# One-hots of the high digit built on partitions from digit rows that DMA spreads, then turned for the histogram

## The chip, the cores and the metric

The kernel runs on one core of a Trainium2 chip. The metric is the device time of one launch in microseconds (us). The engines are named as in the profile: PE is TensorE, DVE is VectorE, ACT is ScalarE, POOL is GpSimd, SP is SyncE. SP computes nothing; it issues DMAs, one after the other, in the order of its program.

## The reference, cut to what matters

2048 users have 200 history entries each, and an entry has three ids (0 to 999), each a row of one of three tables.

```python
ub = jnp.concatenate([table_i1[rec_his[:, :, 0]], table_i2[rec_his[:, :, 1]], table_i3[rec_his[:, :, 2]]], axis=2)
mask = rec_his[:, :, 0] == 0
att_in = jnp.concatenate([q, ub, q - ub, q * ub], axis=-1)
score = ((att_in @ w_att1.T + b_att1) @ w_att2.T + b_att2)[..., 0]
score = jnp.where(mask, 0.0, score)
browse = jnp.einsum('bl,ble->be', score, ub)
```

The score is linear in the history row, so it is a sum of three looked-up numbers per entry, and the weighted sum of rows is a histogram of scores over ids, multiplied by the tables. Behind it come two dense layers with batch statistics and a sigmoid.

## The kernel before, in words

**Lookup by digits.** An id is 25 times a high digit (40 values) plus a low digit (25 values). For 100 entries of one user (half a history) a one-hot of the high digit for three features, 120 wide, with 8 more rows in front, makes 128 (`HJ`). With the table's scores laid out as 128 rows (high digit) by 75 columns (low digit of three features) one matmul group looks all scores of the high digit up into `sel`. The 8 front rows hold the low digit and its square, and `far` rows in `scoretab` turn them into a huge negative number wherever the column is not the entry's low digit, so a maximum over the 25 columns picks the score.

**The histogram** (`add_scores`) is a matmul of the same one-hot, now with the 100 entries on partitions, by the low one-hot times the score in three bf16 parts (`scaled_lo`).

**Two layouts.** The lookup needs the high one-hot with 128 rows on partitions (`hiT`), the histogram with 100 entries on partitions (`onehot_hi`). DVE builds `onehot_hi` with one comparison (`onehot_high`), ACT adds the low-digit columns (`lo_rows`), and SP issues one DMA transpose per step that writes `hiT` (`turn_hi`). The digits themselves reach the 100 partitions by PE transposes of `digits_b` (tasks `digit`, kind 1 the high one, kind 0 the low one).

**Tiles, steps, slots.** A tile is 128 users (16 tiles), a step is 8 users or 16 half histories (16 steps a tile, 256 in all), and a slot is half a step. In a step DVE does `pick` (maximum over `sel`), `onehot_high` for the step two ahead (`AHEAD = 2`), `onehot_low`, the second `pick`, and `scale` for the step before. POOL turns the picked scores into three bf16 parts between `pick` and `scale`. PE does in each slot 24 matmuls of `read_scores`, some task, and 24 matmuls of `add_scores` for the slot `LAG = 5` back. In the last two and the first two steps of a tile SP also moves the next tile's score table (`place_scores`, five chunks of three DMAs each); twice a tile it loads ids (`load_rows`), once it keeps `x1`. All of these stand in SP's one queue with the transposes, and each waits there for its semaphores before the next is looked at.

Of the kernel before, what the change touches and what calls it, by code (L numbers as in the profile page):

```python
# [16 lines left out]
def build(nc, r_user, r_item, r_his, table_user, table_i1, table_i2, table_i3, w_att1, b_att1,  # L17
# [12 lines left out]
    POSP = 112  # L30
# [11 lines left out]
    RING = 6  # L42
# [5 lines left out]
    with ExitStack() as ctx:  # L48
# [16 lines left out]
        onehot_hi = sb("onehot_hi", [POSP, RING, PER, HJ], BF16)  # L65
        onehot_lo = sb("onehot_lo", [POS, 2, PER, NF, LP], BF16)
        scaled_lo = sb("scaled_lo", [POS, 2, PER, 3, U], BF16)
        hiT = sb("hiT", [128, 4, PER * POSP + 128 - POSP], BF16)
# [5 lines left out]
        digits = sb("digits", [POS, 2, 2, 2 * HALF, NF, 2], BF16)  # L74
        far_rows = sb("far_rows", [1, 3, LO], BF16)
# [4 lines left out]
        centre = sb("centre", [POS, 1])  # L80
# [3 lines left out]
        iota_i = sb("iota_i", [POS, HI], I32)  # L84
        iota_hi = sb("iota_hi", [POS, HI], BF16)
# [37 lines left out]
        x1_rows = nc.dram_tensor("x1_rows", [MH, 2, B], F32).ap()  # L123
        stats = raw_f[:, 0:72].rearrange("p (m q s) -> p m q s", m=3, q=4)
# [38 lines left out]
        hi_ready = sem("hi_ready")  # L163
        lo_ready = sem("lo_ready")
        hiT_in = [sem(f"hiT_in{i}") for i in range(4)]
        rim_zero = sem("rim_zero")
# [3 lines left out]
        lo_rows_ready = sem("lo_rows_ready")  # L170
# [33 lines left out]
        def ring_slot(n):  # L204

            return n % 5 if n < STEPS - 1 else RING - 1

        def sums_before(k, n):

            return 2 * k - (8 if 5 <= n < STEPS - 1 else 10 if n < 5 else 2 * STEPS - 2)  # L210

        def ring_used(k, n):

            return not isinstance(k, int) or sums_before(k, n) > 0

        prologue = (["attw"] + [("tableT", i) for i in range(7)] + [("digit", 1, 0), ("digit", 0, 0), "item", "query",
                                                                    "w1T", "w1uT", "w2T"])
        DIGITS0 = prologue.index(("digit", 0, 0)) + 1  # L220
# [8 lines left out]
        def split_bank(first, r):  # L229
# [8 lines left out]
        EVERY = {0: "item", 1: "query", 2: ("digit", 1, 1), 3: ("digit", 0, 1), FIN_SLOT + PARTS - 1: "finish",  # L238
                 FIN_SLOT + PARTS: "layer1", 19: "userT", 20: ("digit", 1, 0), 21: ("digit", 0, 0)}
        IN_FIRST = {s: w for s, w in EVERY.items() if w not in FIN}  # L240
        IN_LAST = {s: w for s, w in EVERY.items() if w not in ("item", "query", ("digit", 1, 0), ("digit", 0, 0))}
# [38 lines left out]
        def _(sp):  # L280
# [25 lines left out]
            sp.wait_ge(far_made, 3)  # L306
            for j in range(NF):
                sp.dma_start(far[0:1, j, :], far_rows[:, 0, :]).then_inc(far_in, 16)
                sp.dma_start(far[1 + 2 * j:2 + 2 * j, j, :], far_rows[:, 1, :]).then_inc(far_in, 16)
                sp.dma_start(far[2 + 2 * j:3 + 2 * j, j, :], far_rows[:, 2, :]).then_inc(far_in, 16)  # L310
# [5 lines left out]

            def turn_hi(t, n):
# [31 lines left out]
            def tile(t, last=False):  # L349
                for n in range(STEPS):  # L350
                    if n == 14 and not last:
                        place_scores(t + 1, 0)
                    if n + AHEAD < STEPS:
                        turn_hi(t, n + AHEAD)
                    elif not last:
                        turn_hi(t + 1, n + AHEAD - STEPS)
                    if n < 2:
                        place_scores(t, 3 + n)
                    if n in (2, 9) and not last:
                        load_rows(2 * t + 2 + n // 9)  # L360
# [8 lines left out]

            load_rows(1)  # L370
            for n in range(AHEAD):
                turn_hi(0, n)
# [12 lines left out]
        def _(pool):  # L385
# [61 lines left out]
            def step(t, n, last=False):  # L447
# [8 lines left out]
                if n == 3:  # L456

                    if not (isinstance(t, int) and t == 0):
                        await_ge(task_full, tasks_start(t) - 2)
                    gather_users(t, 2 * t + (3 if last else 4))  # L460
# [6 lines left out]
            chain(pool.iota(iota_i[:, :], pattern=[[1, HI]], base=1, channel_multiplier=0))  # L467
            chain(pool.tensor_copy(iota_hi[:, :], iota_i[:, :]))
# [7 lines left out]
            pool.tensor_scalar(far_rows[:, 1, :], column, 2.0 * FAR, None, ALU.mult).then_inc(far_made, 1)  # L476
            chain(pool.memset(ids_u[:, TILES:TILES + 1, :].bitcast(F32), 0.0))
# [28 lines left out]
        def _(pe):  # L506
# [6 lines left out]
            def hi_columns(s4, g):  # L513

                return onehot_hi[0:POS, s4, g, :]

            def read_scores(t, s):

                k = t * SLOTS + s
                if s % 2 == 0:  # L520
                    pe.wait_ge(hiT_in[s // 2 % 4], 16 * (t * (STEPS // 4) + s // 8 + 1))
# [6 lines left out]
                for c in range(8):  # L528
# [5 lines left out]
                    rows = hiT[0:HJ, s // 2 % 4, g * POSP:g * POSP + 128]  # L534
# [5 lines left out]
            def add_scores(t, s):  # L540

                k = t * SLOTS + s
                n = s // 2
                pe.wait_ge(scaled_ready, t * STEPS + n + 1)
                if not (isinstance(k, int) and k < 2):
                    pe.wait_ge(wsum_copied, k - 1)
                for i in range(6):
                    for b in range(4):
                        g = (s % 2) * 8 + 2 * b + i // 3
                        mm = pe.matmul(wsum_ps[:, s % 2, b * W:(b + 1) * W].rearrange("p (j v) -> p j v", j=NF),  # L550
                                       hi_columns(ring_slot(n), g),
# [22 lines left out]
            def task(what, seq, t, part=0, parts_n=1):  # L574
# [42 lines left out]
                elif name == "digit":  # L617

                    hb, kind = what[2], what[1]
                    await_ge(digits_b_ready, (t * 2 + hb) * 2 + 2 - kind)  # L620
                    src = digits_b[:, kind, :].rearrange("p (l f) -> p f l", f=NF)
# [35 lines left out]
            def slot(t, s, last=False):  # L657
# [6 lines left out]
                elif s in here:  # L664
                    what = here[s]
                    of = t
                    if what in ("item", "query", ("digit", 1, 0), ("digit", 0, 0)):
# [57 lines left out]
        def _(act):  # L725
# [39 lines left out]
            def task(what, seq, t):  # L765
# [18 lines left out]
                elif name == "digit":  # L784
                    kind, hb = what[1], what[2]
                    if not (isinstance(t, int) and t == 0):

                        if kind == 1:
                            act.wait_ge(hi_ready, (t - 1) * STEPS + 8 * hb + 8)
                        else:  # L790
                            act.wait_ge(lo_ready, (t - 1) * STEPS + 8 * hb + 8)
                    src = misc_b[0:POS, 0:2 * NF * HALF]
                    ins = act.activation(digits[:, hb, kind, :, :, :].rearrange("p g j d -> p j g d"),
# [47 lines left out]
            def lo_rows(t, n):  # L841

                k = t * STEPS + n
                hb, g0 = n // 8, (n % 8) * PER
                if n in (0, 8):

                    if isinstance(t, int) and t == 0 and n == 0:
                        act.wait_ge(task_copied, DIGITS0)
                    elif n == 0:
                        act.wait_ge(task_copied, tasks_start(t))  # L850
                    else:
                        act.wait_ge(task_copied, task_before(t, 3) + 1)

                if ring_used(k, n):
                    act.wait_ge(wsum_full, sums_before(k, n))
                low = digits[:, hb, 0, g0:g0 + PER, :, 0]
                rows = onehot_hi[0:POS, ring_slot(n), :, 1:1 + 2 * NF].rearrange("p g (j i) -> p g j i", i=2)
# [334 lines left out]
```

## Time and profile before

| | |
|---|---|
| median of 3 runs | 1602.13 us (1595.31 to 1602.28) |
| the profiled execution, its own time | 1588.28 us |
| its span | 1586.5 us |
| busy: DVE, PE, POOL, ACT | 1438.8, 1330.5, 1132.5, 716.7 us |
| mean granted clock of PE | 0.921 of full speed |
| DMA | 194.21 MB in 510281 packets |

Busy time counts computing instructions. Instructions that issue DMAs are not in it, so SP has no row in that table, although it can be occupied all the time; its occupation is read from the durations of its DMA instructions (queue SPq). The share of a DMA queue is the time that its packets took, over 16 DMA engines and the stretch; packets that overlap count twice, so it can pass 100%.

### The profile page before, as it was taken

The page shows a single profiled execution, that of the slowest core. Times are in us where ns is not written, and L with a number is a line of the kernel's source. Part 1 is how long each engine was busy: PE and PEld are TensorE (multiplying, and loading weights), DVE is VectorE, ACT ScalarE, POOL GpSimd, SP SyncE. Part 2 cuts the span into 40 slices and gives each one's busy share as a digit, 9 for nine tenths or more (in the row PEclk, how much of TensorE's full clock was granted, in tenths as well). Part 3 has the DMA queues.
Part 4 walks back from the last instruction along what each step waited for, and adds up shares of the span by engine and source line. Part 5 has one row for each costly group of instructions (what it writes and reads, how often), then busy time and mean ns, then how long its engine had stood idle before and what let it go on. Part 6 is the DMA issues. An engine that isn't in the chain of part 4 may idle for free.

```text
span 1586.5 us, 67332 instructions
## 1 busy us (share of the span) xinstructions
PE 1330.5 (84%) x26911; PEld 1225.9 (77%) x26911; DVE 1438.8 (91%) x1453; ACT 716.7 (45%) x1633; POOL 1132.5 (71%) x1669
## 2 busy tenths in 40 slices
PE   5687988889797987979788897988879798997965
PEld 4577878879797877969788797888879787887861
DVE  7799898999999998999989999898999999998955
ACT  5353453535354353635445353443535344452217
POOL 3588586787877777687767878686786878777730
PEclk9799999999999998999899899999989999998966
DMA  2768676585757777585676858486676857678720
GB/s 30 146 109 156 96 145 123 121 158 111 156 108 145 121 129 140 109 158 109 135 116 120 158 111 157 98 139 125 121 157 102 157 106 138 128 124 147 118 68 0
DMA packets 510281, 194.21 MB, mean 122 GB/s; under 512 B 484005, under 2 KB 491797, under 8 KB 510045
## 3 DMA queue, kind: packets, MB, share of 16 engines
q1 hardware_dynamic: 492454, 162.61, 57.8%
q10 hardware_dynamic: 15448, 26.51, 6.5%
q8 instruction: 221, 3.62, 0.9%
q0 software_dynamic: 2144, 1.36, 0.7%
q14 instruction: 14, 0.11, 0.0%
HBM read 8.45 MB, written 1.44 MB: 6 GB/s over the span
## 4 chain that ended last, share of the span: by engine, by line
POOL 62%; issue 24%; PE 4%; DVE 4%; POOLq 2%; DMA 2%; SPq 1%; ACT 1%; ACTq 0%; DVEq 0%
POOL score L431 16%; POOL score L436 14%; POOL score_r L440 10%; POOL parts L441 7%; POOL parts L444 7%; POOL parts L437 4%; POOL item_rows L409 2%; POOL user_rows L417 2%; DMA hiT<-onehot_hi 2%; PE sel L536 1%; PE wsum_ps L550 1%; PE misc L638 1%; DVE score_j L1000 1%; DVE scoretab L1086 1%; PE sel L714 1%
## 5 line engine op out<-in xcount | busy, mean ns | idle before, releaser
L536 PE MATMUL sel<-scoretab,hiT 128*128 128x75 bf16 x12288 | 560.3, 206 | 146.8 <-DMA hiT<-onehot_hi 117.4
L536 PEld LDWEIGHTS sel<-scoretab,hiT 128*128 128x128 bf16 x12288 | 521.4, 103 | 208.6 <-issue 141.7
L550 PE MATMUL wsum_ps<-scaled_lo,onehot_hi 100*128 100x75 bf16 x12288 | 554.3, 204 | 69.6 <-DVE scaled_lo L1012 68.8
L550 PEld LDWEIGHTS wsum_ps<-scaled_lo,onehot_hi 100*128 100x128 bf16 x12288 | 509.1, 102 | 85.9 <-DVE scaled_lo L1012 78.9
L1012 DVE TENSOR_TENSOR scaled_lo<-onehot_lo,parts 100x3744 bf16<-100x3744 bf16 x256 | 539.5, 2107 | 22.0 <-POOL parts L444 19.0
L755 ACT ACTIVATE wsum_ring<-wsum_ps 128x300 f32<-128x300 f32 x512 | 215.0, 420 | 676.0 <-PE wsum_ps L550 666.0
L431 POOL TENSOR_TENSOR score<-score_j 100x16 f32<-100x16 f32 x256 | 306.9, 1199 | 293.6 <-DVE score_j L1000 292.8
L1000 DVE TENSOR_REDUCE score_j<-sel 100x24 f32<-100x600 f32 x512 | 395.8, 773 | 36.5 <-PE sel L536 34.2
L968 DVE TENSOR_TENSOR onehot_hi<-digits,iota_hi 100x1920 bf16<-100x1920 bf16 x256 | 297.8, 1164 | 47.6 <-PE wsum_ps L550 46.9
L762 ACT ACTIVATE scores_b<-acc 128x512 bf16<-128x512 f32 (+1 forms) x318 | 256.1, 805 | 43.8 <-PE acc L569 24.5
L436 POOL TENSOR_TENSOR score<-score,score_j 100x16 f32<-100x16 f32 x256 | 229.3, 896 | 22.0
L986 DVE TENSOR_TENSOR onehot_lo<-digits,iota_lo 100x1248 bf16<-100x1248 bf16 x256 | 211.8, 827 | 0.0
L440 POOL TENSOR_TENSOR score_r<-score,parts 100x16 f32<-100x16 f32 x256 | 168.8, 659 | 20.0
L444 POOL TENSOR_TENSOR parts<-score_r,parts 100x32 bf16<-100x32 f32 x256 | 123.2, 481 | 20.1
L441 POOL TENSOR_TENSOR parts<-score,parts 100x32 bf16<-100x32 f32 x256 | 128.2, 501 | 0.0
L638 PE MATMUL misc<-weightsum,table_blk 128*96 128x128 f32 x800 | 113.9, 286 | 4.6 <-DMA weightsum<-wsum_ring 4.6
L569 PE MATMUL acc<-queryT,tableT 97*128 97x128 f32 x758 | 111.1, 287 | 0.6 <-issue 0.6
L562 PE MATMUL acc<-scores_b,minus_identb 128*128 128x512 bf16 (+1 forms) x212 | 101.5, 479 | 0.1
L638 PEld LDWEIGHTS misc<-weightsum,table_blk 128*96 128x96 f32 x800 | 94.3, 169 | 4.8 <-issue 4.8
L409 POOL DMA_INDIRECT item_rows<-in_L_rec_table_i_dram,ids_now x51 | 81.9, 1605 | 20.5 <-POOL ids_now L403 12.5
L569 PEld LDWEIGHTS acc<-queryT,tableT 97*128 97x128 f32 x758 | 94.0, 193 | 0.7 <-issue 0.7
L858 ACT ACTIVATE onehot_hi<-digits,centre 100x48 bf16<-100x48 bf16 x256 | 91.6, 358 | 0.0
(155 smaller groups left out, 671.0 us busy)
## 6 DMA issues: line engine op xcount, KB each, us to landing
scoretab<-scores_b SPq DMA_DIRECT2D x144, 187.5 KB
weightsum<-wsum_ring ACTq DMA_DIRECT2D x128, 125.0 KB
weightsum<-wsum_ring ACTq DMA_DIRECT2D x64, 150.0 KB
scoretab<-scores_b SPq DMA_DIRECT2D x96, 93.8 KB
raw<-in_r_rec_his_dram SPq DMA_DIRECT2D x32, 150.0 KB
hiT<-onehot_hi SPq DMA_TRANSPOSE x256, 4.8
x_rows<-x_tile SPq DMA_DIRECT2D x14, 100.0 KB
scores_b<-x_rows SPq DMA_DIRECT2D x1, 1400.0 KB
```

The costliest lines, as they stand in the source:

```text
L431: pool.tensor_tensor(score_2[:, :], score_j[:, p2, :, 0], score_j[:, p2, :, 1], ALU.add).then_inc(parts_step, 1)
L436: pool.tensor_tensor(score[:, :], score_2[:, :], third, ALU.add)
L440: pool.tensor_tensor(score_r[:, :], score[:, :], parts[:, p2, :, 0, 0], ALU.subtract)
L441: pool.tensor_tensor(parts[:, p2, :, 1, :], twice(score[:, :]), parts[:, p2, :, 0, :], ALU.subtract).then_inc(parts_step, 1)
L444: pool.tensor_tensor(parts[:, p2, :, 2, :], twice(score_r[:, :]), parts[:, p2, :, 1, :], ALU.subtract).then_inc(parts_ready, 1)
L536: mm = pe.matmul(o, rows, scoretab[0:HJ, s // 16, :, b, i, :], start=(i == 0), stop=(i == 2))
L550: mm = pe.matmul(wsum_ps[:, s % 2, b * W:(b + 1) * W].rearrange("p (j v) -> p j v", j=NF), hi_columns(ring_slot(n), g), scaled_lo[:, n % 2 ...
L638: mm = pe.matmul(misc[0:E, 0:TILE].rearrange("p (w b) -> p w b", w=4), table_blk[:, lo, :, :].rearrange("p j e -> p (j e)"), weightsum[0:H ...
L762: act.activation(scores_b[:, :, stage, slice(*ROUNDS[r])], split_bank(first, r), ACT.Copy).then_inc(split_copied, 1)
L968: dve.tensor_tensor(onehot_hi[0:POS, ring_slot(n), :, HB:].rearrange("p g (j v d) -> p g j v d", j=NF, d=2), digits[:, hb, 1, g0:g0 + PER, ...
L1000: dve.tensor_reduce(score_j[:, n % 2, g0:g0 + 8, :].rearrange("p (q c) j -> p q (c j)", q=2), sel[0:POS, 2 * (s % 2):2 * (s % 2) + 2, 0:4 ...
L1012: ins = dve.tensor_tensor(scaled_lo[:, n % 2, :, :, :].rearrange("p q i (u d) -> p (q i) u d", d=2), onehot_lo[:, n % 2, :, :, :].rearrang ...
```

## The change

1. ACT copies both digits, and the low digit's centred square, from interleaved to feature by feature (`spread_digits`, `digits_f`), and SP stores them in DRAM (`store_digits`, `digit_store`): twice a tile.
2. In each step SP loads each feature's high digit, 1600 numbers, onto 40 partitions at once: three DMAs whose source repeats one row 40 times (`load_high`, `high_rows`).
3. DVE compares each partition with its own number (`high_of`) in one `tensor_scalar`, which gives `hiT` at once, with no transpose.
4. The 6 low-digit rows come by one more DMA from `digit_store` into `hiT` (`load_front`), behind the comparison.
5. The DMA transpose goes the other way, `hiT` to `onehot_hi`, 128 by 2048 instead of 112 by 2048, and is waited for by `add_scores` instead of `read_scores`.
6. `lo_rows` and the PE and ACT tasks for the high digit go away.

```diff
+            def store_digits(h):
+                await_ge(spread_ready, KINDS * (h + 1))
+                sp.dma_start(digit_store[bass.ds(h, 1), :, :, :].rearrange("o r p l -> p (o r) l"),
+                             digits_f[:, :, :, :].rearrange("p k f l -> p (k f) l")).then_inc(rows_out, 16)
+            def load_high(t, n):
+                if n % 8 == 0:
+                    await_ge(rows_out, 16 * (h + 1))
...
+                    await_ge(hi_made, k - 1)
+                users = slice((n % 8) * PER, (n % 8) * PER + PER)
+                for j in range(NF):
+                    sp.dma_start(high_rows[hi_first(j):hi_first(j) + HI, n % 2, :],
+                                 digit_store[bass.ds(h, 1), FEAT[j]:FEAT[j] + 1, users, :].rearrange("o r p l -> (o r) (p l)")
+                                 .to_broadcast([HI, PER * POS])).then_inc(high_in[n % 2], 16)
+            def load_front(t, n):
+                await_ge(hi_made, k + 1)
+                sp.dma_start(hiT[1:1 + 2 * NF, n % RING, :, 0:POS],
+                             digit_store[bass.ds(2 * t + n // 8, 1), NF:KINDS * NF, users, :]
+                             .rearrange("o r p l -> (o r) p l")).then_inc(front_in[n % RING], 16)
             def turn_hi(t, n):
-                await_ge(hi_ready, k + 1)
-                await_ge(lo_rows_ready, k + 1)
-                if not (isinstance(k, int) and k < 4):
-                    await_ge(sel_full, 2 * k - 6)
-                sp.dma_start(hiT[:, n % 4, 0:PER * POSP].rearrange("p (g l) -> p g l", g=PER),
-                             onehot_hi[:, ring_slot(n), :, :].rearrange("p g h -> p (g h)"), transpose=True
-                             ).then_inc(hiT_in[n % 4], 16)
+                await_ge(front_in[n % RING], 16 * (t * (STEPS // RING) + n // RING + 1))
+                if not (isinstance(k, int) and k < RING):
+                    await_ge(wsum_full, 2 * (k - RING) + 2)
+                sp.dma_start(onehot_hi[:, n % RING, :, :], hiT[:, n % RING, :, :].rearrange("p g l -> p (g l)"),
+                             transpose=True).then_inc(hi_in[n % RING], 16)
             def tile(t, last=False):
                 for n in range(STEPS):
+                    for ahead, load in ((AHEAD, load_front), (2 + AHEAD, load_high), (1, turn_hi)):
+                        if n + ahead < STEPS:
+                            load(t, n + ahead)
...
             def onehot_high(t, n):
-                dve.tensor_tensor(onehot_hi[0:POS, ring_slot(n), :, HB:].rearrange("p g (j v d) -> p g j v d", j=NF, d=2),
-                                  digits[:, hb, 1, g0:g0 + PER, :, :].unsqueeze(3)
-                                  .to_broadcast([POS, PER, NF, HI // 2, 2]),
...
+                dve.wait_ge(high_in[n % 2], NF * 16 * (t * (STEPS // 2) + n // 2 + 1))
...
+                dve.tensor_scalar(hiT[:, n % RING, :, 0:POS], high_rows[:, n % 2, :].rearrange("p (g l) -> p g l", g=PER),
+                                  high_of[:, 0:1], None, ALU.is_equal).then_inc(hi_made, 1)
```

On SP, a step in the middle of a tile's loop body was this before (ISA and REGISTER_ALU rows are waits and the arithmetic for them and for addresses):

```order
L284 REGISTER_ALU
L284 ISA [waits hi_ready,lo_rows_ready]
L324 DMA_TRANSPOSE hiT<-onehot_hi 128x16x112 [waits sel_full]
L284 ISA
L315 ISA [waits digits_b_ready]
L315 DMA raw<-in_r_rec_his_dram 128x300
```

and the same place now reads:

```order
L342 ISA [waits hi_made]
L342 DMA hiT<-digit_store 6x16x100
L333 ISA [waits hi_made]
L333 DMA high_rows<-digit_store 40x1600
L333 ISA
L333 DMA high_rows<-digit_store 40x1600
L333 ISA
L333 DMA high_rows<-digit_store 40x1600
L281 ISA [waits front_in3]
L352 DMA_TRANSPOSE onehot_hi<-hiT 128x16x128 [waits wsum_full]
L313 ISA [waits digits_b_ready]
L313 DMA raw<-in_r_rec_his_dram 128x300
```

Every step has four DMAs more in SP's queue, ahead of the transpose.

On DVE, the inside of a step was this before:

```order
L1000 TENSOR_REDUCE score_j<-sel 100x24 [waits sel_full]
L968 TENSOR_TENSOR onehot_hi<-digits,iota_hi 100x16x120 [waits wsum_full]
L986 TENSOR_TENSOR onehot_lo<-digits,iota_lo 100x1248 [waits scaled_ready]
L1000 TENSOR_REDUCE score_j<-sel 100x24 [waits sel_full]
L1012 TENSOR_TENSOR scaled_lo<-onehot_lo,parts 100x3744 [waits wsum_full,parts_ready,lo_ready]
```

and is this now:

```order
L1023 TENSOR_REDUCE score_j<-sel 100x24 [waits sel_full]
L995 TENSOR_SCALAR hiT<-high_rows,high_of 128x16x100 [waits hi_in1,sel_full,high_in1]
L1009 TENSOR_TENSOR onehot_lo<-digits,iota_lo 100x1248 [waits scaled_ready]
L1023 TENSOR_REDUCE score_j<-sel 100x24 [waits sel_full]
L1035 TENSOR_TENSOR scaled_lo<-onehot_lo,parts 100x3744 [waits wsum_full,parts_ready,lo_ready]
```

The order is the same, but the comparison has another form, 1600 instead of 1920 numbers a partition, and waits for two kinds of DMA (`high_in`, `hi_in`) where it waited for PE.

## Rows read from the trace of the kernel before

**Rows 1.** The page: span, and busy time of each engine.
```profile
span 1586.5 us, 67332 instructions
PE 1330.5 (84%) x26911; PEld 1225.9 (77%) x26911; DVE 1438.8 (91%) x1453; ACT 716.7 (45%) x1633; POOL 1132.5 (71%) x1669
```

**Rows 2.** The page's groups: busy us, mean ns of one | idle before, its releaser.
```profile
L536 PE MATMUL sel<-scoretab,hiT 128*128 128x75 bf16 x12288 | 560.3, 206 | 146.8 <-DMA hiT<-onehot_hi 117.4
L1012 DVE TENSOR_TENSOR scaled_lo<-onehot_lo,parts 100x3744 bf16<-100x3744 bf16 x256 | 539.5, 2107 | 22.0 <-POOL parts L444 19.0
L1000 DVE TENSOR_REDUCE score_j<-sel 100x24 f32<-100x600 f32 x512 | 395.8, 773 | 36.5 <-PE sel L536 34.2
L968 DVE TENSOR_TENSOR onehot_hi<-digits,iota_hi 100x1920 bf16<-100x1920 bf16 x256 | 297.8, 1164 | 47.6 <-PE wsum_ps L550 46.9
L986 DVE TENSOR_TENSOR onehot_lo<-digits,iota_lo 100x1248 bf16<-100x1248 bf16 x256 | 211.8, 827 | 0.0
```

**Rows 3.** Who waited for whom: us in total, times, longest.
```profile
PE sel L536 <- DMA hiT<-onehot_hi: 117.4, 85, 6.1
DVE onehot_hi L968 <- PE wsum_ps L550: 46.9, 57, 1.3
DVE score_j L1000 <- PE sel L536: 34.2, 21, 8.0
```

**Rows 4.** Line 1025 (a tensor_scalar): ns min/median/max, first and last start.
```profile
L1025 DVE TENSOR_SCALAR digit_hi<-raw_f x32: 298/301/318, 12.9 to 1415.4; 128x300 bf16<-128x300 f32 x32
```

**Rows 5.** SP's queue by line: ns min/median/max of issuing one, starts.
```profile
L324 SPq DMA_TRANSPOSE hiT<-onehot_hi x256: 1462/1588/4878, 41.1 to 1510.5; - x128
DMA to landing us min/median/max: 3.9/4.8/6.9
...
L340 SPq DMA_DIRECT2D scoretab<-scores_b x240: 706/758/1722, 45.1 to 1446.3; - x120
...
L315 SPq DMA_DIRECT2D raw<-in_r_rec_his_dram x31: 339/918/1201, 16.3 to 1401.8; - x31
L315 SPq FUSED_REGOPS  x28: 51/51/54, 156.6 to 1401.6; - x28
L315 SPq MOVE raw<-in_r_rec_his_dram x28: 29/34/43, 156.7 to 1401.7; - x28
...
L347 SPq DMA_DIRECT2D x_rows<-x_tile x14: 916/922/1095, 209.2 to 1411.0; - x14
```

**Rows 6.** SP's queue in order of time, 600 to 620 us: start, us.
```profile
603.71 2.62 SPq L340 DMA_DIRECT2D scoretab<-scores_b  x3
606.75 2.36 SPq L324 DMA_TRANSPOSE hiT<-onehot_hi  x1
609.31 2.91 SPq L340 DMA_DIRECT2D scoretab<-scores_b  x3
612.66 3.98 SPq L324 DMA_TRANSPOSE hiT<-onehot_hi  x1
```

**Rows 7.** Timeline, 600 to 625 us: PE's longest pause there.
```profile
622.05 1.70 PE L536 MATMUL sel<-scoretab,hiT 128*128 128x75 bf16 x24 [5.41 <-DMA hiT<-onehot_hi]
```

**Rows 8.** DMA queues, whole span: packets, MB, share (q1 is SP's, q10 ACT's).
```profile
q1 hardware_dynamic: 492454, 162.61, 57.8%
q10 hardware_dynamic: 15448, 26.51, 6.5%
```

**Rows 9.** DMA queues, 640 to 650 us: transposes only.
```profile
q1 hardware_dynamic: 3648, 0.92, 48.3%
```

**Rows 10.** DMA queues, 606 to 608 us: the score table only.
```profile
q1 hardware_dynamic: 97, 0.37, 57.5%
```

**Rows 11.** DMA queues, 8 to 12 us: table_blk, 128-byte packets from DRAM.
```profile
q1 hardware_dynamic: 2974, 0.38, 60.1%
```

More of the change, by code:

```diff
@@ L202, in hi_first @@
             return HB + j * HI
[L204 to L218, printed above, removed]
+        prologue = (["attw"] + [("tableT", i) for i in range(7)] + [("digit", 0), "item", "query",
                                                                     "w1T", "w1uT", "w2T"])
-        DIGITS0 = prologue.index(("digit", 0, 0)) + 1
+        DIGITS0 = prologue.index(("digit", 0)) + 1
         ITEM0 = prologue.index("item") + 1
@@ L368, in tile @@
                         place_scores(t + 1, n - 13)
+            store_digits(0)
             load_rows(1)
+            for n in range(2):
+                load_high(0, n)
             for n in range(AHEAD):
-                turn_hi(0, n)
+                load_front(0, n)
+                load_high(0, 2 + n)
+            turn_hi(0, 0)
             for c in range(3):
@@ L533, in read_scores @@
                     g = (s % 2) * 8 + c
-                    rows = hiT[0:HJ, s // 2 % 4, g * POSP:g * POSP + 128]
+                    rows = hiT[:, s // 2 % RING, g, :]
                     for i in range(3):
@@ L666, in slot @@
                     of = t
-                    if what in ("item", "query", ("digit", 1, 0), ("digit", 0, 0)):
+                    if what in ("item", "query", ("digit", 0)):
                         of = t + 1
@@ L839, in scale_raw, with spread_digits @@
                                ).then_inc(raw_f_ready, 1)
[L841 to L857, printed above, removed]
-                act.activation(rows[:, :, :, 0], low, ACT.Identity, bias=centre[:, :])
-                act.activation(rows[:, :, :, 1], low, ACT.Square, bias=centre[:, :]).then_inc(lo_rows_ready, 1)
+            def spread_digits(h):
+                act.wait_ge(digits_b_ready, 2 * (h + 1))
+                if not (isinstance(h, int) and h == 0):
+                    act.wait_ge(rows_out, 16 * h)
+                high, low = (digits_b[:, kind, :].rearrange("p (l f) -> p f l", f=NF) for kind in (1, 0))
+                act.activation(digits_f[:, 0, :, :], high, ACT.Copy).then_inc(spread_ready, 1)
+                act.activation(digits_f[:, 1, :, :], low, ACT.Copy).then_inc(spread_ready, 1)
+                act.activation(digits_f[:, 2, :, :], low, ACT.Square, bias=centre[:, :]).then_inc(spread_ready, 1)
             def slot(t, s, last=False):
@@ L874, in slot @@
                     copy_sums(t - 1, s - LAG + SLOTS)
-                ahead = s // 2 + AHEAD
-                if s % 2 == 0 and ahead < STEPS:
-                    lo_rows(t, ahead)
-                elif s % 2 == 0 and not last:
-                    lo_rows(t + 1, ahead - STEPS)
+                if s == 1:
+                    spread_digits(2 * t + 1)
+                if s == 18 and not last:
+                    spread_digits(2 * t + 2)
                 if s in (4, 5, 6) and not (isinstance(t, int) and t == 0):
@@ L905, in _ @@
                 task(prologue[seq], seq, 0)
-            for n in range(AHEAD):
-                lo_rows(0, n)
             scale_raw(1)
```

143 lines of the change are left out of this document (83 added, 60 removed).

## The prediction

> **What bounds the kernel now.** I read the busy times first: DVE is busy for 1438.8 of 1586.5 us, PE for 1330.5 [rows 1]. By groups a DVE step is scale 2.11, two picks of 0.77, the high one-hot 1.16 and the low one-hot 0.83 us [rows 2], together 5.64 us, and 256 of them make 1444. So DVE sets the pace, PE is close behind. The waits say where DVE still stands idle: 46.9 us in front of the high one-hot, 34.2 us for `sel` [rows 3]. Behind the latter stands PE, which waited 117.4 us in 85 places for the turned one-hot `hiT` [rows 3]; the longest pauses, such as 5.41 us, come when SP has the score table to move as well [rows 7]. There the reader should look at SP: two groups of three table DMAs took 2.62 and 2.91 us to issue, and the transposes between and behind them 2.36 and 3.98 us [rows 6]. SP is an engine with a throughput too.
>
> The pace of a tile is read from the DMA that keeps `x1`, once a tile: (1411.0 - 209.2) / 13 = 92.4 us, or 5.78 us a step [rows 5]. The rest of the span is the prologue and the dense tail. The profiled execution took 1588.3 us, 0.9% less than the median shown; sums below are made against 1588.
>
> **The change part by part.**
>
> *DVE.* The comparison goes from a `tensor_tensor` of 1920 numbers (1.16 us) to a `tensor_scalar` of 1600. The trace has one `tensor_scalar`: 300 numbers from f32 to bf16 in 0.301 us [rows 4]. The two-input comparisons cost 0.00050 us a number and 0.20 fixed at most (from 1248 numbers in 0.827 and 1920 in 1.164) [rows 2]. If the new form runs at the rate of the old one it takes 0.2 + 0.8 = 1.0 us; if the 0.301 us is nearly all fixed and it runs twice as fast, 0.2 + 0.4 = 0.6 us. I take 0.6. DVE's step falls to 5.08 us, and by 0.56 * 256 = 143 us in all; with the slow form by 41 us.
>
> The Trainium skill (VectorE: DVE Perf Modes, the perf-mode tier table) says that a bf16 `tensor_scalar` in SBUF runs in the 4x mode and a `tensor_tensor` in 2x at most. By it, 1600 numbers are an estimated 0.42 us and a fixed part, which agrees with the lower value. No row here shows a bf16 one.
>
> *PE and ACT.* Off ACT go two small activations a step; ACT is busy for 716.7 us [rows 1], so this is worth nothing. Three PE transposes per half tile go too: nothing. PE's wait for `hiT` moves: `read_scores` now needs the comparison and then a small load (`load_front`), `add_scores` needs the transpose, two and a half steps later. The transpose's 4.8 us to landing [rows 5] leave the short path. By itself that could give back most of the 117 us.
>
> *SP's queue.* This is what the change pays with. A step had one transpose; it has one transpose and four plain DMAs. Issue costs, from [rows 5]: the transpose 1.59 us for 112 rows, and I scale it with the rows to 1.59 * 128 / 112 = 1.81; the three loads on 40 partitions like the score table's, which go to 40 partitions too, 3 * 0.758 = 2.27; `load_front` (96 pieces) like the `x1` DMA (200 pieces), 0.92; an address computed per DMA 0.051 + 0.034, four times 0.34. Three satisfied waits with their arithmetic take 606.75 - 603.71 - 2.62 = 0.42 us [rows 6]; now there are four, 0.56. The step is 1.81 + 2.27 + 0.92 + 0.34 + 0.56 = 5.90 us, against DVE's 5.08. A tile is 16 * 5.90 = 94.4; 15 score table DMAs at 0.758 and five gaps of 0.2 add 12.4; two id loads at 0.918, two stores and an `x1` DMA at 0.92, and their waits add 5.3. Sum 112.1 us a tile, against 92.4. Nothing hides this: SP takes its queue in order, the step's first wait is for the comparison two steps ahead, and the comparison waits for loads that SP issued two steps before. DVE, PE and POOL then stand idle a few tenths of a microsecond to a few microseconds a step.
>
> Bounds: at the minima of [rows 5] (1.46; 3 * 0.706; 0.34 for `load_front`) with the same waits, a step is 4.82 us and a tile 16 * 4.82 + 15 = 92, no slower than now. With transposes stretched as in [rows 6] by about 1 us in every step, a tile is 128 us.
>
> *The DMA engines.* They stay below SP, but not far. Transposes alone: 3648 packets in 48.3% of 10 us [rows 9] are 755 a microsecond, so 128 * 16 packets take 2.71 us (1792 took 2.37). The loads: 3 * 40 * 3200 bytes = 384 KB; the score table, also on 40 partitions, moves 0.37 MB in 2 us with 57.5% of the engines' time [rows 10], so they take 2.1 us, every step. `load_front` is 96 packets; 2974 small ones took 60.1% of 4 us on 16 engines [rows 11], 13 ns each, and on 6 engines that is 0.2 us. ACT's own DMAs are 6.5% of the span [rows 8], 0.40 us a step. The store, 1152 packets twice a tile at 13 to 27 ns, is 0.2. Together 5.6 us a step; with the score table (2.30 MB a tile at 0.184 MB a us, 12.5 us) a tile is 102 us.
>
> The Trainium skill (DMA: Bandwidth & Descriptors, why a DMA increments its semaphore by 16 and not by 1) speaks against the change here: a DMA runs on the largest number of engines, up to 16, that divides its slowest dimension, so 40 partitions get 10 engines and 6 get 6. The 57.5% of the score table's stretch agrees with ten of sixteen. By it the loads always burden the same ten engines, which the transposes need too.
>
> *Prologue and end.* The first store, loads and comparison lie beside the splitting of the first scores; a few microseconds more, inside the range.
>
> **Sum.** 1588 + 16 * (112.1 - 92.4) = 1903 us. I say 1900.
>
> **The rivals.**
>
> - *DMA engines bind, SP doesn't.* If the plain DMAs issue in half the time assumed, SP's tile is under 100 us and the DMA engines' 102 decides: 1588 + 16 * (102 - 92.4) = 1742. For it: an id load issued in 0.339 us at best [rows 5]. Against it: the 40-partition ones never under 0.706.
> - *Faster.* Issue at the minima, and the loads faster than the score table's: then DVE decides again, 1588 - 143 = 1445, and PE's busy 1330 us with its warm pauses lies just below. It decides if SP's step stays under 5.1 us with the table chunks absorbed by the two steps of lead, and the ten engines too. Against it: both sums above pass it, separately.
> - *No change.* SP's and the engines' tile at 92: 1588.
> - *Worse than the sum.* Transposes back-pressured as in [rows 6] while the three loads sit in the rings, or PE pausing so often that its clock falls (its 24 matmuls took 1.70 us behind the 5.41 us pause [rows 7]): 128 us a tile, 1588 + 16 * 35.6 = 2158.
>
> **How the numbers follow.** SP binds as summed, 1800 to 2050: 0.50. DMA engines bind, 1640 to 1800: 0.20. Faster, about 1445: 0.15. No change (0.5% is about what a measurement of this kernel can tell): 0.04. Worse, above 2050: 0.11. The range 1570 to 2160 leaves out the faster case and a rest of the last, 0.2 together. Faster 0.15, same 0.04, slower 0.81.
>
> **What would show it.** In the changed kernel's trace: the `tensor_scalar` near 0.6 us, so DVE's busy time near 1300; DVE waiting for `high_rows` in most steps, where it waited for PE; SP's queue without gaps, its starts of one line 6 us or more apart in the quiet steps; the three loads at 0.75 us or more each; the `x1` DMA every 112 us; PE's clock about as before, since its pauses are short. The prediction is wrong if SP's queue shows gaps in which it waits for the comparison while DVE is busy throughout (then issue was cheaper), or if the loads land late although SP is idle (then the DMA engines bind), or if the comparison runs at 1 us or more.

## The result and the profile after

The changed kernel takes 1986.62 us (median of 4 runs, 1984.63 to 1987.32), the kernel before 1598.72 (1584.97 to 1602.28): 1.2455 times as long by the comparison of the runs, with an interval of 1.2405 to 1.2505 (the two medians divide to 1.243). Slower was forecast, 1900 us; the range 1570 to 2160 holds the time. Below, a kernel's time is the median of all its executions, while the ratios leave out those in the chip's slower state (two of four in e3, one each in e4, e11 and e12), and as e4's trace is of such a one, the table has no intervals for it.

The page of the changed kernel, its busy times, and the chain of work that ended last, by line:

```profile
span 1985.5 us, 70413 instructions
PE 1423.6 (72%) x26815; PEld 1322.4 (67%) x26815; DVE 1321.0 (67%) x1451; ACT 606.0 (31%) x1185; POOL 1072.0 (54%) x1675
...
SPq 70%; issue 15%; PE 7%; DMA 4%; DVE 2%; ACT 1%; ACTq 1%; POOL 0%; DVEq 0%; POOLq 0%
SPq L352 38%; SPq L333 13%; SPq L367 9%; SPq L342 5%; PE sel L578 2%; PE wsum_ps L594 2%; DMA hiT<-digit_store 2%; SPq L281 1%; PE misc L681 1%; SPq L283 1%; SPq L318 1%; SPq L374 1%; SPq L313 1%; DMA raw<-in_r_rec_his_dram 1%; DVE scoretab L1109 1%
```

DVE has less to do than before, 1321.0 against 1438.8 us [rows 1], and is idle a third of the span. 70% of the chain is SP's queue, and its transposes (L352) are 38%. Three groups of that page answer to [rows 2]; who waited for whom answers to [rows 3]:

```profile
L1023 DVE TENSOR_REDUCE score_j<-sel 100x24 f32<-100x600 f32 x512 | 398.6, 778 | 561.7 <-PE sel L578 561.2
L1009 DVE TENSOR_TENSOR onehot_lo<-digits,iota_lo 100x1248 bf16<-100x1248 bf16 x256 | 210.2, 821 | 0.0
L995 DVE TENSOR_SCALAR hiT<-high_rows,high_of 128x1600 bf16<-128x1600 bf16 x256 | 161.2, 630 | 37.2 <-DMA high_rows<-digit_store 31.2
```

```profile
DVE score_j L1023 <- PE sel L578: 561.2, 281, 11.4
...
PE sel L578 <- DMA hiT<-digit_store: 355.4, 100, 10.4
...
PE sel L578 <- DMA scoretab<-scores_b: 118.7, 15, 14.6
```

The comparison costs 0.630 us instead of 1.164. Its loads are rarely late (31.2 us in all). DVE waits for PE, and PE for the six front rows (355.4 us) and for the score table (118.7): DMAs that come late because they stand in SP's queue. SP itself hardly waits any more. What it waited for longest in total inside the tiles was this before:

```profile
SPq L286 <- DVE onehot_hi L968: 517.2, 181, 5.4
```

and is this now:

```profile
SPq L342 <- DVE hiT L995: 12.3, 4, 11.1
```

SP's queue by line (ns min/median/max of issuing one), against [rows 5]:

```profile
L352 SPq DMA_TRANSPOSE onehot_hi<-hiT x256: 1771/3236/9981, 40.5 to 1919.4; - x128
DMA to landing us min/median/max: 4.3/6.4/12.1
```

```profile
L333 SPq DMA_DIRECT2D high_rows<-digit_store x768: 281/287/1842, 23.2 to 1900.6; - x192
```

```profile
L342 SPq DMA_DIRECT2D hiT<-digit_store x256: 279/302/1952, 37.6 to 1915.7; - x128
```

```profile
L374 SPq DMA_DIRECT2D x_rows<-x_tile x14: 961/966/975, 244.8 to 1792.6; - x14
```

The plain DMAs from DRAM onto 40 and 6 partitions are cheap to issue, 0.29 and 0.30 us, and the transpose takes 3.24 us of SP where 1.59 was usual. The `x1` DMA gives the pace: (1792.6 - 244.8) / 13 = 119.1 us a tile, against 92.4.

SP's queue in order of time, in quiet steps and across the end of a tile:

```profile
802.58 0.28 SPq L342 DMA_DIRECT2D hiT<-digit_store  x1
803.12 1.24 SPq L333 DMA_DIRECT2D high_rows<-digit_store  x3
804.70 3.26 SPq L352 DMA_TRANSPOSE onehot_hi<-hiT  x1
808.29 0.29 SPq L342 DMA_DIRECT2D hiT<-digit_store  x1
...
850.45 3.60 SPq L352 DMA_TRANSPOSE onehot_hi<-hiT  x1
854.39 4.85 SPq L367 DMA_DIRECT2D scoretab<-scores_b  x6
859.60 0.30 SPq L342 DMA_DIRECT2D hiT<-digit_store  x1
860.17 1.23 SPq L333 DMA_DIRECT2D high_rows<-digit_store  x3
861.77 2.83 SPq L352 DMA_TRANSPOSE onehot_hi<-hiT  x1
864.85 3.03 SPq L367 DMA_DIRECT2D scoretab<-scores_b  x3
871.40 0.30 SPq L342 DMA_DIRECT2D hiT<-digit_store  x1
```

The first quiet step shown is 5.7 us of SP's time, with no gap but the satisfied waits and the arithmetic between two DMAs. The last steps of a tile have the table's DMAs on top, 3 to 5 us more, and behind the tile's last one stands a pause of 3.52 us, 867.88 to 871.40. It is the loop's branch (L413), as the chain of that stretch shows:

```profile
868.02 0.06 SPq L413
868.07 2.97 issue
871.04 0.06 SPq L413
```

To see where in a tile the time goes, I took the starts of the 256 high comparisons, and the mean interval from that of step n to that of step n+1 over tiles 1 to 14. Those with n = 1 to 5 lie where the table is moved (the comparison runs two steps ahead, so they hold a tile's last step and the next one's first four); the other eleven are the quiet part.

| us a tile | n = 1 to 5 | other eleven | tile |
|---|---|---|---|
| before | 28.9 | 63.6 | 92.5 |
| changed | 48.4 | 70.5 | 118.9 |

Of the 26.4 us that a tile lost, 19.5 fall on these five intervals. Three of the quiet ones, n = 8 to 10, are not SP's: PE is busy throughout them, and they take 6.08, 6.06 and 7.19 us here and the same within 0.01 in e1, e3, e9 and e10 (6.10, 6.93 and 5.22 before). So about 1 us a tile of the quiet part's loss is PE's, and no relief of SP below gives it back.

### The profile page after: what moved, and what is told of

It reads as the page before. It is cut to its first block, busy times and chain, and to the rows that moved or that the text cites. A ratio compares the mean times of both kernels' runs of the same rounds, so it can differ in the third digit from the quotient of the medians.

```text
span 1985.5 us, 70413 instructions
## 1 busy us (share of the span) xinstructions
PE 1423.6 (72%) x26815; PEld 1322.4 (67%) x26815; DVE 1321.0 (67%) x1451; ACT 606.0 (31%) x1185; POOL 1072.0 (54%) x1675
## 4 chain that ended last, share of the span: by engine, by line
SPq 70%; issue 15%; PE 7%; DMA 4%; DVE 2%; ACT 1%; ACTq 1%; POOL 0%; DVEq 0%; POOLq 0%
SPq L352 38%; SPq L333 13%; SPq L367 9%; SPq L342 5%; PE sel L578 2%; PE wsum_ps L594 2%; DMA hiT<-digit_store 2%; SPq L281 1%; PE misc L681 1%; SPq L283 1%; SPq L318 1%; SPq L374 1%; SPq L313 1%; DMA raw<-in_r_rec_his_dram 1%; DVE scoretab L1109 1%
## 5 line engine op out<-in xcount | busy, mean ns | idle before, releaser
L578 PE MATMUL sel<-scoretab,hiT 128*128 128x75 bf16 x12288 | 622.9, 217 | 485.4 <-DMA hiT<-digit_store 355.4
L578 PEld LDWEIGHTS sel<-scoretab,hiT 128*128 128x128 bf16 x12288 | 580.4, 110 | 547.7 <-issue 483.4
L468 POOL TENSOR_TENSOR score<-score_j 100x16 f32<-100x16 f32 x256 | 261.5, 1021 | 753.3 <-DVE score_j L1023 753.1
L594 PE MATMUL wsum_ps<-scaled_lo,onehot_hi 100*128 100x75 bf16 x12288 | 599.2, 212 | 12.8 <-issue 10.6
L594 PEld LDWEIGHTS wsum_ps<-scaled_lo,onehot_hi 100*128 100x128 bf16 x12288 | 554.6, 107 | 21.3 <-issue 14.4
L473 POOL TENSOR_TENSOR score<-score,score_j 100x16 f32<-100x16 f32 x256 | 348.3, 1361 | 22.0
L995 DVE TENSOR_SCALAR hiT<-high_rows,high_of 128x1600 bf16<-128x1600 bf16 x256 | 161.2, 630 | 37.2 <-DMA high_rows<-digit_store 31.2
L474 POOL TENSOR_TENSOR parts<-score,score_j 100x32 bf16<-100x32 f32 x256 | 134.5, 525 | 0.0
L477 POOL TENSOR_TENSOR score_r<-score,parts 100x16 f32<-100x16 f32 x256 | 95.7, 374 | 20.0
L481 POOL TENSOR_TENSOR parts<-score_r,parts 100x32 bf16<-100x32 f32 x256 | 75.6, 295 | 20.0
```

The source lines that it names most:

```text
L468: pool.tensor_tensor(score_2[:, :], score_j[:, p2, :, 0], score_j[:, p2, :, 1], ALU.add).then_inc(parts_step, 1)
L473: pool.tensor_tensor(score[:, :], score_2[:, :], third, ALU.add)
L578: mm = pe.matmul(o, rows, scoretab[0:HJ, s // 16, :, b, i, :], start=(i == 0), stop=(i == 2))
```

## The experiments

Theory R (rings) says that the loads' bytes keep ten DMA engines full, and that this reaches SP as a longer issue of the transposes. Theory S says that SP's own time decides, by the number and kind of its DMAs. B and Q are about the boundary. The table gathers all runs; issue is the transpose's median on SP. The text goes through them one by one.

| run | time us | ratio to before (interval) | issue us | n = 1 to 5 | other eleven |
|---|---|---|---|---|---|
| changed | 1986.6 | 1.2455 (1.2405 to 1.2505) | 3.24 | 48.4 | 70.5 |
| e1 short loads | 1815.5 | 1.1378 (1.1336 to 1.1420) | 2.07 | 43.6 | 64.9 |
| e2 table first | 2004.7 | 1.2544 (1.2471 to 1.2616) | 3.29 | 49.9 | 70.9 |
| e3 SP unrolled | 1874.2 | 1.1779 (1.1704 to 1.1854) | 3.36 | 42.8 | 67.2 |
| e4 loads on ACT | 2008.2 | 1.2561 (1.2446 to 1.2677) | | | |
| e5 loads 32 + 8 | 2133.5 | 1.3382 (1.3298 to 1.3466) | 2.69 | 50.8 | 78.0 |
| e9 half transpose | 1723.2 | 1.0820 (1.0752 to 1.0889) | 1.29 | 37.8 | 64.0 |
| e10 table on ACT | 1966.6 | 1.2278 (1.2196 to 1.2360) | 3.62 | 47.5 | 70.4 |
| e12 both | 1937.5 | 1.2133 (1.2045 to 1.2222) | 3.87 | 46.2 | 68.3 |
| e6 before + loads | 1835.9 | 1.1495 (1.1410 to 1.1580) | 2.13 | 41.6 | 67.4 |
| e7 before + tiny loads | 1749.7 | 1.0990 (1.0918 to 1.1063) | 1.57 | 38.9 | 64.2 |
| e11 before, table on ACT | 1670.5 | 1.0450 (1.0385 to 1.0514) | 1.59 | 33.7 | 63.1 |
| e13 e11 unrolled | 1670.3 | 1.0493 (1.0430 to 1.0556) | 1.56 | 34.5 | 63.2 |

**e1, the loads' bytes taken away.**

```diff
                 users = slice((n % 8) * PER, (n % 8) * PER + PER)
+                users = slice((n % 8) * PER, (n % 8) * PER + 2)
...
-                    sp.dma_start(high_rows[hi_first(j):hi_first(j) + HI, n % 2, :],
+                    sp.dma_start(high_rows[hi_first(j):hi_first(j) + HI, n % 2, 0:2 * POS],
...
-                                 .to_broadcast([HI, PER * POS])).then_inc(high_in[n % 2], 16)
+                                 .to_broadcast([HI, 2 * POS])).then_inc(high_in[n % 2], 16)
...
```

> The changed kernel with the three loads of a step moving 200 numbers a partition instead of 1600 (48 KB instead of 384 KB a step); the rest of the rows keeps a constant, so the one-hots are not those of the reference. The same number of instructions on every engine. Theory R (rings): the transposes take 3.24 us of SP's time each, against 1.77 at their shortest, because the loads' bytes keep ten DMA engines busy and the transpose cannot be handed over sooner. Then the median issue of a transpose falls below 2.1 us, SP is idle part of every step, and the time falls to 1600 to 1700. Theory S (SP's own cost): a transpose of 128 rows in the new direction costs SP 3.2 us whatever else is moved. Then its issue stays above 3.0 us and the time above 1930.

The transposes' median issue fell from 3.24 to 2.07 us:

```profile
L353 SPq DMA_TRANSPOSE onehot_hi<-hiT x256: 1604/2072/10094, 40.2 to 1748.0; - x128
```

Theory R is right on the issue, and S's claim that a transpose costs 3.2 whatever else is moved falls. But R's time was missed: it fell by 171 us to 1815, not to the 1600 to 1700 expected: without the bytes the eleven quiet intervals are nearly back (64.9 against 63.6), while the five at the boundary keep 43.6 against 28.9.

**e9, half of each transpose.**

```diff
-                sp.dma_start(onehot_hi[:, n % RING, :, :], hiT[:, n % RING, :, :].rearrange("p g l -> p (g l)"),
-                             transpose=True).then_inc(hi_in[n % RING], 16)
+                sp.dma_start(onehot_hi[:, n % RING, 0:PER // 2, :],
+                             hiT[:, n % RING, 0:PER // 2, :].rearrange("p g l -> p (g l)"), transpose=True).then_inc(hi_in[n % RING], 16)
...
-                                       onehot_hi[0:POS, n % RING, g, :],
+                                       onehot_hi[0:POS, n % RING, g % 8, :],
...
```

> The changed kernel with only half of each transpose done (8 of 16 blocks; the histogram reads the first 8 twice, so its sums are not the reference's). It sizes the transpose in SP's queue: at 3.24 us for the whole its issue falls to about 1.6, the quiet step from 6.35 to under 5.2, where DVE decides, and the time to 1650 to 1750. If the loads alone made the queue late, the transpose's halving would leave it above 1900.

```profile
L352 SPq DMA_TRANSPOSE onehot_hi<-hiT x256: 1231/1294/5154, 40.8 to 1646.4; - x128
```

Inside its forecast: 263 us less. It has all loads and all DMAs, and the transpose costs SP 1.9 us a step less. It halves both the transpose's bytes and its share of SP's time, so it sizes the transpose and does not tell the two apart.

**e3, SP's loop written out.**

```diff
-            with sp.Fori(1, TILES - 1) as t:
+            for t in range(1, TILES - 1):
                 tile(t)
```

> The changed kernel with SP's loop over tiles written out, so without the pause of 3.5 us behind the loop's branch (13 of them in the trace), and without the arithmetic and the extra semaphore instruction at each wait. If SP's time is what decides (its queue without gaps), the 13 pauses give back 46 us and 0.3 to 0.4 us a step another 60 to 90: 1850 to 1900. If the DMA engines decide and SP only passes their pace on, the saved issue time comes back as longer transposes and the time stays above 1940.

112 us less by the medians (the two fastest executions took 1854 and 1866 us), with the same bytes and the same DMAs, as S expected. The interval with the pause (n = 3) went from 8.77 to 5.75 us, and the rest of a tile lost 5.9 us. Since only SP's branch, arithmetic and extra semaphore instructions were taken away, SP's time does decide; the transposes' issue hardly rose (3.36), so little of what was saved came back as back-pressure.

**e7 and e6, the kernel before with three more DMAs a step.**

```diff
+            def extra_loads(t, n):
+                q = t * (STEPS // 2) + n // 2
+                if not (isinstance(q, int) and q == 0):
+                    await_ge(spare_in[n % 2], NF * 16 * q)
+                for j in range(NF):
+                    src = his_flat[bass.ds((t * STEPS + n) * 800, 16)].rearrange("(o x) -> o x", o=1)
+                    sp.dma_start(spare[n % 2, hi_first(j):hi_first(j) + HI, 0:16],
+                                 src.to_broadcast([HI, 16])).then_inc(spare_in[n % 2], 16)
...
+                    extra_loads(t, n)
                     if n + AHEAD < STEPS:
                         turn_hi(t, n + AHEAD)
```

(e6 has 800 for 16; `spare` lies in DRAM.)

> The same with 16 numbers a row instead of 800: SP issues as many DMAs, the bytes are gone. Theory R: the transposes' issue stays at 1.6 us, and the time within 1.5% of the kernel before, since SP's step of 1.6 + 3 * 0.4 + 0.8 = 3.6 us lies under the 5.8 us of a step. If the count of DMAs in SP's queue costs by itself, it is as slow as with the full rows.

> The kernel before, with three loads more in every step ahead of the transpose, of the changed kernel's size (40 rows of 3200 bytes from one row of DRAM, here into a scratch tensor in DRAM that nobody reads). Theory R: the bytes alone stretch the transposes' issue from 1.59 us to over 2.5 and slow the kernel by 5 to 15%, to 1680 to 1850. If bytes are harmless and only the new chain through the loads costs, it stays below 1640.

e7's forecast by R was wrong: DMAs that move next to nothing cost 9.9%. The transposes' issue stayed at 1.57 us, as R said. SP's queue in e7 across a boundary:

```profile
869.70 2.53 SPq L354 DMA_DIRECT2D scoretab<-scores_b  x3
873.01 2.49 SPq L339 DMA_DIRECT2D spare<-in_r_rec_his_dram  x3
875.92 1.55 SPq L326 DMA_TRANSPOSE hiT<-onehot_hi  x1
877.81 2.44 SPq L354 DMA_DIRECT2D scoretab<-scores_b  x3
880.55 2.47 SPq L339 DMA_DIRECT2D spare<-in_r_rec_his_dram  x3
883.42 1.57 SPq L326 DMA_TRANSPOSE hiT<-onehot_hi  x1
885.19 3.76 SPq L354 DMA_DIRECT2D scoretab<-scores_b  x3
889.31 2.47 SPq L339 DMA_DIRECT2D spare<-in_r_rec_his_dram  x3
892.18 1.55 SPq L326 DMA_TRANSPOSE hiT<-onehot_hi  x1
```

Steps of 7.5 and 8.8 us, from transpose to transpose (875.92, 883.42, 892.18): three small groups and no gap as long as 1 us. My expectation had summed only the quiet step. The quiet intervals are untouched (64.2 against 63.6), the five at the boundary took 38.9 against 28.9. This is half of the changed kernel's loss there, with next to no bytes. (The extra DMAs issue at 0.73 us each, against 0.29 for the changed kernel's loads; a step's DMAs take SP 3.76 us in e7 and 4.40 in the changed kernel.) e6 adds the bytes: 86 us more than e7, 2.6 a tile at the boundary and 3.2 in the quiet part. Its time lies in R's range, but the issue, 2.13 us, falls short of the 2.5 expected.

**e5, the same bytes on more engines.**

```diff
                 for j in range(NF):
-                    sp.dma_start(high_rows[hi_first(j):hi_first(j) + HI, n % 2, :],
+                    for r0, r1 in ((0, 32), (32, HI)):
+                        sp.dma_start(high_rows[hi_first(j) + r0:hi_first(j) + r1, n % 2, :],
...
```

> The changed kernel with each load on 40 partitions split in two, 32 and 8 partitions: six DMAs a step of the same bytes. Where a DMA runs on the most engines up to 16 that divide its partitions, 40 use 10 engines with 4 rows each, and 32 and 8 together use 16, with at most 3 rows each. Theory R (DMA engines back up into SP): the fullest engine carries 9 rows a step instead of 12, the transposes issue faster, and the time falls by 30 to 100 although SP has three DMAs more. Theory S (SP's count of instructions): three more at 0.29 + 0.19 are 1.4 us a step, and the time rises by 200 or more.

```profile
L353 SPq DMA_TRANSPOSE onehot_hi<-hiT x256: 1588/2692/10075, 42.6 to 2070.7; - x128
```

Both theories at once: spread bytes shorten the transposes' issue by 0.54 us, and three more DMAs cost more than that; S gave the direction, though the time rose by 147 us and not by 200. The Trainium skill (DMA: Bandwidth & Descriptors, why a DMA increments its semaphore by 16 and not by 1) says that a DMA runs on the largest number of engines, up to 16, that divides its slowest dimension; the shorter issue agrees with it, but which engines a DMA used is not in these traces.

**e4, the loads issued by ACT.**

```diff
-                    for ahead, load in ((AHEAD, load_front), (2 + AHEAD, load_high), (1, turn_hi)):
+                    for ahead, load in ((AHEAD, load_front), (1, turn_hi)):
...
+                if s % 2 == 1:
+                    ahead = s // 2 + 2 + AHEAD
+                    if ahead < STEPS:
+                        load_high_act(t, ahead)
...
```

> The changed kernel with the three loads of a step issued by ACT instead of SP (the first four steps' loads still by SP). The same bytes on the same DMA engines. If SP's issue time decides, SP's step loses 1.23 us and some arithmetic, and the time falls by 1.5 * 240 = 360 at most, held by DVE at about 1650 to 1750. If the DMA engines decide, only the queue's order changes: above 1900.

No gain, 2008 us. Three DMAs fewer on SP did not pay. Its trace has room in SP's queue again:

```profile
SPq L283 <- DVE hiT L1014: 282.2, 130, 4.4
```

while single transposes held SP for up to 12.5 us and took up to 24.6 to land. That the same bytes met the transposes from a second queue fits this, but ACT, which now issues 756 loads between its copies of the sums, may also have been late, and no run separates the two.

**e2, the table ahead in the queue.**

```diff
-                    for ahead, load in ((AHEAD, load_front), (2 + AHEAD, load_high), (1, turn_hi)):
+                    for ahead, load in ((AHEAD, load_front), (0, "place"), (2 + AHEAD, load_high), (1, turn_hi)):
...
```

> The changed kernel with the score table's DMAs at a tile's end and start put ahead of the step's three loads and its transpose in SP's queue (behind the small front load). Theory B (order at the tile's boundary): part of the loss is that the table's chunks now stand behind loads and a transpose, where the first stood ahead before. Then PE's 118.7 us of waiting for the table falls below 50 us and the time falls by 40 to 120, to 1870 to 1950. Rival: SP's queue is full, and what is put ahead only makes the rest late; then PE waits for the front rows instead, and the time stays within 1% of 1987.

The rival held. The waits say what the order buys and what it costs:

```profile
PE sel L579 <- DMA hiT<-digit_store: 450.5, 120, 10.8
DVE score_j L1024 <- PE sel L579: 415.9, 250, 10.5
DVE hiT L996 <- DMA high_rows<-digit_store: 206.6, 79, 6.4
...
PE sel L579 <- DMA scoretab<-scores_b: 45.3, 14, 14.7
```

PE's wait for the table did fall below 50 us, from 118.7 to 45.3, as theory B said. But the high rows' loads, late by 31.2 us in the changed kernel, are now late by 206.6, and the front rows by 95 us more. The time stayed within 1% (18 us above), so the order gains nothing: what is put ahead in this queue makes the rest late.

**e10 to e13, the table issued by ACT**, in the changed kernel and in the one before, with SP's loop or written out.

```diff
+                if s in (0, 2):
+                    place_scores(t, 3 + s // 2)
+                if s == 28 and not last:
+                    place_scores(t + 1, 0)
+                    place_scores(t + 1, 1)
+                if s == 30 and not last:
+                    place_scores(t + 1, 2)
...
```

> The changed kernel with the score table's DMAs (15 a tile) issued by ACT instead of SP; same bytes, same loads, same transposes. Four steps around a tile's boundary take 12.9, 8.8, 10.4 and 10.6 us in the changed kernel, where the same four took 5.4 to 7.2 before. Theory Q (SP's queue at the boundary): there SP has 6 or 3 table DMAs on top of a step's 6 us, 2.3 to 4.9 us more, and is late for everything behind. Then the four fall to 6 to 8 us each, a tile loses 12 to 19 us and the time falls to 1700 to 1800. Theory R (the DMA engines are full at the boundary): the table's 2.3 MB must still pass the same ten engines beside loads and transposes, and the time stays above 1900.

> The same with SP's loop over tiles written out as well. Writing it out alone gave 113 us. If both mend the same thing (SP's backlog at the boundary), little is added to the table's move, less than 50 us; if SP decides in quiet steps too, it adds 60 or more.

> The kernel before with the score table's DMAs issued by ACT. Theory Q says that the same queue costs the kernel before too: PE waited 117 us for turned one-hots, most of it where SP's transposes stand behind table DMAs. Then the time falls by 20 to 80, to 1520 to 1580. If that wait comes from the table's bytes, or only fills time in which DVE is late anyway, the time stays within 0.5%; if ACT, held up by 0.7 us a DMA, frees the sums late, it gets slower.

> The same with SP's loop written out. In the kernel before SP is idle between transposes in the quiet steps, so this should add nothing measurable: within 0.5% of the one before it.

Theory Q, that SP's backlog of table DMAs alone makes the boundary slow, fell. e10 gives 1%, and in the kernel before the move costs 4.5%. SP's queue in e10 shows what came in place of the backlog:

```profile
868.38 4.12 SPq L333 DMA_DIRECT2D high_rows<-digit_store  x3
872.88 13.70 SPq L352 DMA_TRANSPOSE onehot_hi<-hiT  x1
890.08 0.28 SPq L342 DMA_DIRECT2D hiT<-digit_store  x1
```

One transpose held SP for 13.70 us while the table's DMAs from ACT ran, and the longest took 27.3 us to land, against 12.1 in the changed kernel. e11 has no loads, and its transposes come late too:

```profile
L324 SPq DMA_TRANSPOSE hiT<-onehot_hi x256: 1462/1592/7870, 41.1 to 1581.9; - x128
DMA to landing us min/median/max: 3.9/4.5/14.8
```

against 4.88 and 6.9 us [rows 5]. The two maxima lie in the first tile; in the loop's tiles they are 5.12 and 14.5 us, against 3.98 and 6.8 before. In one queue the table's DMAs are spaced by SP's issue between two transposes; from a second queue they run beside a transpose under way. The Trainium skill (DMA: Bandwidth & Descriptors, issuing engines are not separate DMA queues) says that DMAs of all engines run on the same 16 and interleave; the late transposes of e10 and e11 agree. Writing out the loop gives 29 us on top of e10 (e12), less than the 50 that was set as the limit: by that, most of it mends the same thing as the table's move, though in e12 the transposes' issue also rose, to 3.87 us. In e13 it gives nothing that the intervals tell from e11, as expected. ACT is held up too by its DMAs (69.9 us before its copies of the sums, 9.8 in the kernel before, have no releaser but issue). How the 4.5% divides between ACT and the transposes no run separates, but the waits of e11 speak for the transposes as the larger part:

```profile
PE sel L530 <- DMA hiT<-onehot_hi: 174.6, 77, 10.4
DVE score_j L1016 <- PE sel L530: 120.2, 59, 8.5
...
PE wsum_ps L544 <- ACT wsum_ring L749: 7.8, 4, 2.1
```

The first two were 117.4 and 34.2 us before [rows 3].

No version beat the kernel before.

## Why the prediction was right, and where its terms were not

- **DVE.** 0.6 us was taken for the comparison, 0.630 measured. Its busy time fell by 118 us, and the span did not follow: DVE was idle a third of the time. The value of 0.6 was chosen between 0.6 and 1.0. (The trace before had more than one `tensor_scalar`; the others read and wrote f32.) The Trainium skill (VectorE: DVE Perf Modes, the perf-mode tier table) has a bf16 `tensor_scalar` in its 4x mode, by which 1600 numbers are an estimated 0.42 us and a fixed part; 0.630 agrees, with 0.21 for that part.
- **SP's queue binds: right.** 70% of the chain is SP, which waited about 13 us for the comparison in the whole kernel, and e3 shows it by the time that leaves with SP's own instructions alone, e7 by what tiny DMAs cost.
- **The terms of the SP sum were mis-sized, in both directions.** The three loads: 2.27 us predicted, 3 * 0.287 = 0.86 measured. I took the score table's row for them since both go to 40 partitions; a partition count did not fix the issue time. `load_front`: 0.92 predicted, 0.302 measured. The transpose: 1.81 predicted, 3.24 measured. The errors nearly cancel: 5.00 and 4.40 us a step. Waits and arithmetic, put at 0.34 + 0.56, took the remaining 1.3 us of the 5.71 us step shown above, so the step of 5.90 was close by three errors that offset each other. That is luck.
- **"The DMA engines stay below SP": the step that failed.** The sum kept the engines out of SP's time, with a transpose scaled by its rows alone to 1.81 us; only the rival *Worse than the sum* had the transposes back-pressured, at 0.11. The loads reach SP through the transpose's issue: e1 takes seven eighths of their bytes away, and the issue falls from 3.24 to 2.07 us and the time by 171. Both limits act at once: taking the bytes away (e1) or SP's own instructions (e3) gives back a part each.
- **The boundary.** The sum gave a tile 112.1 us, against 119.1 measured. By its terms the five intervals at the boundary hold 5 * 5.90, the table's 12.4 and about 2 of the 5.3 us of other DMAs, 44 us, and measured 48.4; the other eleven hold 68 and measured 70.5. The loop's pause, 3.5 us behind the branch in each of 13 turns, was in no term; with the loop written out (e3) the interval that holds it was 3.0 us shorter.
- **What was expected of the trace.** Wrong: that DVE would wait for `high_rows` in most steps. It did in 40 of 256, and stood before `sel` instead, for 561 us, since the front rows are the later DMA. Wrong too: three loads at 0.75 us or more each, where 0.29 was measured. Wrong also: a steady clock. The mean granted clock fell from 0.921 to 0.831; after a pause such as this one it was at half, 1.2 GHz (0.50 in the stretch from 859 to 860 us), and 24 matmuls took 1.70 us instead of the 1.01 that they took from 865.01 on:

```profile
858.64 1.70 PE L578 MATMUL sel<-scoretab,hiT 128*128 128x75 bf16 x24 [7.27 <-DMA scoretab<-scores_b]
...
865.01 1.01 PE L578 MATMUL sel<-scoretab,hiT 128*128 128x75 bf16 x24
```

PE's busy time grew by 93 us, though its matmuls for the high digit went away. How much of the kernel's time the lower clock cost, no run separates.

**What was paid for what.** The change frees DVE of 0.53 us a step, 137 us in all by the comparison's own durations, and takes the transpose off the lookup's path. It pays with four DMAs a step in the one queue that had room only in the quiet steps, 384 KB a step on DMA engines that the transposes alone kept busy for 48.3% before [rows 9], and a transpose one seventh larger. The transpose did not get shorter by going the other way; it stayed the largest item of SP's time.

## What to carry to other kernels

Sum the queue that issues DMAs like an engine, step by step and at the busiest place of the loop, not as a mean: here the quiet steps had room and the boundary had none, and three DMAs of 64 bytes a row in each step cost 10%. The issue time of a DMA transpose was not its own cost alone here: it followed the bytes beside it (3.24 us, and 2.07 without most of them), and moving other DMAs to another queue stretched it further (3.62 in e10) and cost the kernel before 4.5%. Before a DVE instruction is replaced by DMA traffic, ask which DMAs will stand ahead of those that PE waits for.

## What the runs showed of the hardware that was not expected

- A DMA from one DRAM row repeated onto 40 partitions is issued by SP in 0.287 us, one between 40 partitions of SBUF in 0.71, and one from a DRAM row onto 40 rows of DRAM in 0.73 (e7).
- SP paused behind the branch of its loop, for 2.9 to 3.4 us from branch to next instruction in all 13 turns of the changed kernel, and for 0.24 to 0.27 in the kernel before. The number of DMAs in the body does not decide it: e7's body has 82 and pauses for 0.28 us at most, and e10's has 85 and pauses for 2.8 us at least, up to 9.7. The bodies that pause have more instructions of SP in the trace: 340 (e10) and 371 (the changed kernel), against 144 (before), 207 (e4) and 280 (e7). The queue of SP's instruction packets moved 81 packets in the changed kernel and in e10, 14 before, 16 in e4 and e7, and 26 with the loop written out (e3), which points to code being fetched again on each turn. That is argued from the counts, not shown.
- A DMA transpose of 128 x 2048 held SP for 1.77 to 9.98 us in the changed kernel, for 1.59 at the least with the loads spread (e5) and for 15.2 at the most with the table from ACT (e12), by what else was in flight.
